# Batch 5's softmax exponentials moved ahead of a middle product, batch 6's joined with batch 7's, in the drain of a conv stage

## The reference, cut to what matters

```python
def _route(x2d, gate_w, num_experts, top_k):
    scores = jax.nn.softmax((x2d @ gate_w.T).astype(jnp.float32), axis=1)
    top_scores, sel = jax.lax.top_k(scores, top_k)
...
    routed_in = (x2d[token_idx].astype(jnp.float32) * top_scores[:, None]).astype(x.dtype)
...
            h = jax.nn.silu(xe @ w1[e]) * (xe @ w3[e])
            out = out + h @ w2[e]
...
x = _layernorm(x + _L0_attn_ref(x, ...), axis=-1)
x = _layernorm(x + _L0_ffn_ref(x, ...), axis=-1)
x = _layernorm(x + _L1_attn_ref(x, ...), axis=-1)
x = _layernorm(x + _L1_ffn_ref(x, ...), axis=-1)
```

## Time and profile before

| | us |
|---|---|
| median of 3 runs | 357.55 |
| lowest, highest | 356.74, 360.23 |
| span of the profiled execution | 349.4 |
| PE busy | 315.8 (90% of the span) |
| DVE busy | 252.3 (72%) |
| ACT busy | 192.7 (55%) |
| POOL busy | 154.6 (44%) |

### The profile page before, as it was taken

How to read it: one execution, slowest core, us unless ns; L and a number is a source line. 1 busy time by engine, 2 the same in 40 slices (tenths; PEclk the granted TensorE clock), 3 DMA queues, 4 the chain that set the end, 5 groups by cost and what they waited for, 6 DMA issues and landing times.

```text
span 349.4 us, 9149 instructions
## 1 busy us (share of the span) xinstructions
PE 315.8 (90%) x2896; PEld 285.2 (82%) x2896; DVE 252.3 (72%) x850; ACT 192.7 (55%) x401; POOL 154.6 (44%) x225
## 2 busy tenths in 40 slices
PE   2989999979689999998977899999889999999992
PEld 2878989868678999998975677777678999999992
DVE  3748988874888568678772589888995787667744
ACT  3154776644464455454536456664557766767342
POOL 0014577862465745876588645312120433134210
PEclk9999999996699999999999699999999999999999
DMA  7991001120134725222501300000000000000001
GB/s 189 421 406 57 17 31 34 38 64 23 46 76 112 234 62 181 63 60 58 160 25 33 122 0 4 2 3 4 1 2 0 3 15 16 15 15 0 18 18 34
DMA packets 17052, 23.24 MB, mean 67 GB/s; under 512 B 3440, under 2 KB 14448, under 8 KB 16224
## 3 DMA queue, kind: packets, MB, share of 16 engines
q1 hardware_dynamic: 14016, 17.84, 16.7%
q0 software_dynamic: 2272, 4.69, 4.0%
q10 hardware_dynamic: 720, 0.14, 0.2%
HBM read 16.93 MB, written 6.73 MB: 68 GB/s over the span
## 4 chain that ended last, share of the span: by engine, by line
PE 55%; DVE 13%; issue 4%; ACT 3%; POOL 2%; DMA 1%; POOLq 0%; DVEq 0%; SPq 0%
PE ps L2015 8%; PE ps L2016 8%; PE ps L1642 6%; PE ps L1845 5%; PE ps L1644 4%; PE ps L1643 4%; PE ps L2079 3%; PE ps L1834 3%; PE ps L1959 2%; PE ps L1937 2%; PE ps L1946 2%; PE ps L1976 2%; DVE sb_stage L1343 1%; DMA out<-sb_work 1%; ACT sb_stage L752 1%
## 5 line engine op out<-in xcount | busy, mean ns | idle before, releaser
L2015 PE MATMUL ps<-sb_w_hi,sb_fh_hi 128*128 128x256 f32 x256 | 61.2, 283 | 1.3 <-DVE sb_w_lo L932 0.6
L2016 PE MATMUL ps<-sb_w_lo,sb_fh_hi 128*128 128x256 f32 x256 | 59.8, 278 | 0.0
L2015 PEld LDWEIGHTS ps<-sb_w_hi,sb_fh_hi 128*128 128x128 f32 x256 | 48.2, 188 | 2.4 <-issue 1.1
L2016 PEld LDWEIGHTS ps<-sb_w_lo,sb_fh_hi 128*128 128x128 f32 x256 | 48.2, 188 | 0.0
L479 POOL DMA_INDIRECT routed<-sb_rows_of,sb_row x32 | 32.3, 1010 | 16.6 <-issue 10.2
L1642 PE MATMUL ps<-sb_w_hi,sb_rT_hi 128*128 x78 | 30.2, 387 | 4.8 <-ACT sb_stage L752 2.7
L619 POOL TENSOR_TENSOR sb_w_lo<-sb_x_in,sb_w_hi 128x256 fp32r<-128x256 f32 x24 | 17.5, 757 | 34.9 <-DVE sb_w_hi L1586 34.9
L1845 PE MATMUL ps<-sb_w,sb_stage 128*128 x234 | 32.8, 276 | 0.0
L571 POOL DMA_INDIRECT answers<-sb_stage x24 | 24.0, 999 | 15.3 <-ACT sb_stage L758 9.4
L1845 PEld LDWEIGHTS ps<-sb_w,sb_stage 128*128 128x128 f32 x234 | 29.2, 191 | 0.2
L463 POOL TENSOR_TENSOR sb_veps_h<-sb_mv_h,sb_eps 128x2 f32<-128x2 f32 x16 | 4.6, 285 | 53.7 <-DVE sb_mv_h L945 48.3
(11 more groups left out here) (301 smaller groups left out, 930.2 us busy)
## 6 DMA issues: line engine op xcount, KB each, us to landing
sb_stage<-in_w SPq DMA_DIRECT2D x2, 1408.0 KB, 13.8
sb_stage<-routed SPq DMA_DIRECT2D x24, 65.0 KB
sb_w<-in_w SPq DMA_DIRECT2D x1, 1536.0 KB, 20.0
sb_x_in<-in_x_tok SPq DMA_DIRECT2D x1, 1024.0 KB, 9.5
sb_x_in<-in_ff_h SPq DMA_DIRECT2D x1, 1024.0 KB
sb_xT_in<-in_ff_h SPq DMA_DIRECT2D x1, 1024.0 KB
sb_got_first<-answers SPq DMA_DIRECT2D x4, 256.0 KB, 3.7
sb_w<-answers SPq DMA_DIRECT2D x4, 256.0 KB, 3.3
```

The source lines that it names most:

```text
L2015: mm(dst, w_hi, x_hi, start=start, stop=False)
L2016: last = mm(dst, w_hi, x_lo, start=False, stop=stop and exact)
```

## The change

It does four things. The two buffers get halves, `below_of[:, b % 2]` and `exps_by[:, b % 2]`, and the waits that guard them become one batch looser. On ACT `exps_of(5)` goes from behind gate row 0 to behind high row 0, with a Silu of one element behind it, and `exps_of(6)` goes from behind `x1_of(6)` to just ahead of `exps_of(7)`. On DVE `weigh(5)` goes from behind `residual(7)` to ahead of `gated_row(0)`, and `weigh(6)` from behind `first_shares()` to behind `share_rest()`. On POOL the four scatters of batch 5 go ahead of `first_root(7)`. PE's and SP's lists are as they were. The new line at 763 moves the lines of ACT and DVE behind it on by one.

```diff
@@ -198,8 +198,8 @@
-        below = sb("below", [P, TILES, EXPERTS])
-        exps = sb("exps", [P, TILES, EXPERTS])
+        below_of = sb("below", [P, 2, TILES, EXPERTS])
+        exps_by = sb("exps", [P, 2, TILES, EXPERTS])
@@ -511,8 +511,8 @@
             first_root(6)
+            scatter_some(5, range(0, 4))
             first_root(7)
-            scatter_some(5, range(0, 4))
@@ -712,8 +712,8 @@
                     act.wait_ge(g0["below"], b + 1)
-                    wait(act, g0["score"], b)
-                    nc.scalar.activation(exps[:, :, :], below[:, :, :], ACT.Exp).then_inc(g0["exps"], 1)
+                    wait(act, g0["score"], b - 1)
+                    nc.scalar.activation(exps_by[:, b % 2, :, :], below_of[:, b % 2, :, :], ACT.Exp).then_inc(g0["exps"], 1)
@@ -759,13 +759,13 @@
             hidden_rows(7)
             high_row(0)
+            exps_of(5)
+            nc.scalar.activation(touched[:, :], ones[:, 0:1], ACT.Silu)
             mid_of(7)
             high_row(1)
             gate_row(0)
-            exps_of(5)
             high_row(2)
             x1_of(6)
-            exps_of(6)
             gate_row(1)
@@ -774,6 +774,7 @@
             high_row(5)
+            exps_of(6)
             exps_of(7)
             gate_row(4)
@@ -1052,8 +1053,8 @@
-                wait(dve, g0["exps"], b)
-                V.tensor_tensor(below[:, :, :], top[:, :, :], top[:, :, 0:1].to_broadcast([P, TILES, EXPERTS]),
+                wait(dve, g0["exps"], b - 1)
+                V.tensor_tensor(below_of[:, b % 2, :, :], top[:, :, :], top[:, :, 0:1].to_broadcast([P, TILES, EXPERTS]),
@@ -1356,9 +1357,9 @@
             low_row(1)
+            weigh(5)
             gated_row(0)
             residual(7)
-            weigh(5)
             low_row(2)
@@ -1370,7 +1371,6 @@
             first_shares()
-            weigh(6)
             low_row(4)
@@ -1379,6 +1379,7 @@
             place(7)
             share_rest()
+            weigh(6)
             gated_row(4)
             turned_row(2)
             weigh(7)
```

More of the change, by code:

```diff
@@ L1223, in weigh @@
                 dve.wait_ge(g0["exps"], b + 1)
-                V.reduce_sum(denom[:, :], exps[:, :, :], axis=AX.X).then_inc(g0["weigh"], 1)
+                V.reduce_sum(denom[:, :], exps_by[:, b % 2, :, :], axis=AX.X).then_inc(g0["weigh"], 1)
                 dve.wait_ge(g0["weigh"], 2 * b + 1)
@@ L1227, in weigh @@
                 dve.wait_ge(g0["weigh"], 2 * b + 2)
-                V.tensor_tensor(rows_by_k[:, b, :, :, AT_SCORE], exps[:, :, 0:TOP_K],
+                V.tensor_tensor(rows_by_k[:, b, :, :, AT_SCORE], exps_by[:, b % 2, :, 0:TOP_K],
                                 rdenom[:, :].unsqueeze(2).to_broadcast([P, TILES, TOP_K]), ALU.mult).then_inc(g0["score"], 1)
```

## The result

The changed kernel takes **362.44 us** (median of 4 runs, 360.70 to 364.55) and the kernel before, in the same rounds, 357.14 us (353.03 to 360.23). The ratio is 1.019 with a 95% interval of 1.011 to 1.027: slower, by about 5 us. The forecast was 356.5, in a range of 354.9 to 358.9. The profiled execution spans 360.7 us and took 362.56.

The account below looks back on a forecast made before the run. VectorE was taken to bound the conv drain, with ScalarE's gate row not setting the pace. Terms -1.06 + 0 + 0, about -1.1, applied to the 357.55 us median gave 356.5, in a range of 354.9 to 358.9.

Parts of the forecast that it names:

- Basis: Whole kernel: summed change applied to the 357.55 us median of runs, 8.15 above the 349.4 us profiled span.
- Exponentials of batch 5 ahead of the middle product: ScalarE, 76.69 to 79.69 us: two table loads, exponentials and touch make `mid_of(7)` 0.25 late; taken as 0.
- Gate row 1, up product 2: Drain on ScalarE and TensorE: gate row near 86.5 instead of 89.27, product near 87.35 instead of 90.02; not the gain.
- Low row 3 bound by VectorE: Drain on VectorE: stays at 90.39 behind work that nothing shortens, so the 2.7 us at TensorE is no gain.
- Term 1, the rank product's wait: VectorE at 92.25 us: its 1.06 us wait for TensorE's batch 6 rank product goes; -1.06, bounds 0 to -1.54.
- clock rival: TensorE's clock low from 92 to 100 us, giving 357.5 (chance 0.18), or still low at 101, giving 359.3 to 361.1 (0.07).
- PE's level eats the gain: TensorE's clock low from 92 to 100 us slows products and transposes, leaving gain 0: 357.5 us, chance 0.18.
- Scatters of batch 5 ahead of root 7: GpSimd from 82.0 us: root begins 0.6 to 1.1 late, its reader ready near 88.2; 0, at worst +0.1.
- Scatters of batches 6 and 7: GpSimd, 100.6 to 109.5 us, at most 110.8: later, but landed by 112 to 113.2, before the 114.4 load; price 0.
- The slower one: TensorE's clock stays low past up product 5, at 101 us, for one or two expert steps: 359.3 to 361.1, chance 0.07.
- Late scatters hold row tile 15: SyncE's load 15 slips if the last scatter lands after about 114.4; 3 us late would end at 359.5, chance 0.03.
- the rivals near 357.5: Cases where no gain remains: low clock (0.18), gain given back or never there (0.10), a drain behind each table load (0.02).

Follow-up runs that it names:

- whole_b: The changed kernel, unchanged, run beside the kernel before on a second chip of the second kind: 362.24 us, ratio 1.0192.
- pool_back: The changed kernel with root 7 ahead of batch 5's scatters on GpSimd again, chip of the second kind: 361.55 us, 1.0195 of the kernel before.
- whole: The changed kernel, unchanged, run again on a chip of the second kind: 362.92 us, 1.0235 of the kernel before.
- burst8: The kernel before plus one GpSimd wait, so batches 6 and 7 push eight in a row; second kind of chip: 362.71 us, 1.0164.
- late6_b: The kernel before with buffer halves and batch 6's exponentials and weighing late, batch 5 as before; second kind of chip: 361.86 us, 1.0183.
- again_b: The kernel before, unchanged, on a chip of the second kind: 356.09 us, 1.0026.
- again: The kernel before, unchanged, on a chip of the first kind: 348.10 us, 1.0015.
- halves: The kernel before with only the buffers' halves and looser waits, all orders as before; first kind of chip: 347.75 us, 1.0005.
- before_gaps: The kernel before plus GpSimd waits for a down product at every second of the first 15 answers' pushes: 357.21 us, 1.0021.
- whole_gaps: The changed kernel plus GpSimd waits between batch 6's and 7's pushes and among the answers' pushes: 359.96 us, 1.0105 of the kernel before.
- whole_pairs: The changed kernel plus GpSimd pauses of about 1.5 us after every second push of batches 6, 7 and first 15 answers: 363.11 us, 1.0236.
- the two parts: The kernel before with buffer halves plus batch 5's edits alone, or batch 6's alone; first kind of chip: 347.80 us (1.0023) and 347.86 us (0.9992).
- early5: The kernel before with buffer halves and batch 5's exponentials, weighing and scatters early, batch 6 as before; first kind of chip: 347.80 us, 1.0023.
- late6: The kernel before with buffer halves and batch 6's exponentials and weighing late, batch 5 as before; first kind of chip: 347.86 us, 0.9992.
- before_pairs: The kernel before plus GpSimd pauses of about 1.5 us after every second push of batches 6, 7 and first 15 answers: 358.18 us, 1.0075.

## Why the prediction was wrong, step by step

- **Basis.** The prediction added the median's distance to the profiled span, 8.15 us, to its sum. That was no constant. In the later runs the time is 1.8 to 2.0 us above its own span (362.56 and 360.7 after); the other 6.3 are most likely the difference of two kinds of chips, since the profile shows no held signal and the runs' times are those of the second kind. The forecast moved a sum made on one kind of chip to the other, and only the sum of the first was worked out. The starting point itself was good (357.55, and 357.14 in the rounds of the result); what failed is the change's own sum, -1.1 for about +5.3.
- **Exponentials of batch 5 ahead of the middle product: right.** Worked out 79.69 for `mid_of(7)` against 79.30 measured, with the whole stretch 0.3 us early. The touch took 0.20, a load 1.28, and the next instruction came 0.01 to 0.02 behind it. The Trainium skill (ScalarE: Activation LUTs, "What ACT_TABLE_LOAD costs") would add a drain of about 1.38 to each load; it is not there.
- **Gate row 1, up product 2: right.** 85.34 for 86.5, and 86.45 for 87.35; the gap of 2.72 is 0.43.
- **Low row 3 bound by VectorE: right in kind.** It came at 89.66, not at 90.39, and row transpose 4 at 90.08 instead of 90.8, waiting 1.49 for it.
- **Term 1, the rank product's wait: right that it goes, not shown as a gain.** VectorE read it at 91.22 with no idle time. Up product 6 is at 101.30 where 102.3 was forecast and 103.39 was before: -2.1 instead of -1.06, of which 0.3 was there at the drain's start and 0.4 more came with low row 3. Most of it goes with TensorE's level, as the last point but one of this list shows.
- **TensorE's level:** 1.00 granted in 100 to 103, and from 82.9 to 106.8 without a break, so in this execution neither clock rival happened up to there. In `whole_b` it is 0.50 from 90.3 to 97.1, which is the rival "PE's level eats the gain". In the changed kernel it is 0.50 again from 106.8 to 117.0, after TensorE had stood for 2.54 us behind a held signal; the step from row transpose 9 to 10 takes 3.9 us there, for 2.8 before. So about 1 us of the loss goes with the level, as a consequence of the hold.
- **Scatters of batch 5 ahead of root 7: right in the places, wrong in "0, at worst +0.1".** First at 81.55 (82.0 forecast), root 7 at 86.40, ending at 87.40, and its reader `first_norm(7)` starts at 87.43. The prediction took the reader to be ready only near 88.2, as before. When the stretch ahead of it runs quicker, the reader is ready first, and the root, behind four pushes, is what it waits for. VectorE in `whole_b`:

```profile
87.63 0.60 DVE L1281 TENSOR_SCALAR sb_rows_of<-sb_work,sb_mv_odd,sb_rstd_odd 128x128 f32<-128x128 f32 x2 [2.42 <-POOL sb_rstd_odd L466]
```

  Six of the ten profiles with the new order have this wait, 1.2 to 2.4 us; none of the ten with the old order has it. In time it can't be told: `pool_back` (1.0195) and `whole` (1.0235) have intervals that overlap.
- **Scatters of batches 6 and 7: the step that failed.** Their places were foreseen well: first at 99.57 for 100.6, last at 108.47 for 109.5. "If the eight then follow each other without the pause between batches" stands in the prediction, and is priced only by when their data must be in. "Price 0" is wrong by the other thing that they do on these chips: while GpSimd pushes without a pause, most signals of TensorE don't land. `burst8` puts the price of joining the two runs of four at 1.64% (0.93 to 2.35), about 5.8 us, and `late6_b` at 1.83%. The changed kernel's whole loss (1.9%, 2.35% and 1.9% in its three measurements) is that, with nothing over that these can tell.
- **The rivals.** The slower one named the clock, and 359.3 to 361.1; the time was over it and by another mechanism. "Late scatters hold row tile 15" had the right instructions and the wrong mechanism: no row transpose waited for them at 114.
- **Where the 2.1 us of the drain went.** They can't be put down to the change. From row transpose 0 to 8 the changed kernel takes 27.7 us and the kernel before 29.4, but TensorE's level is low for 3.4 us of the one and 13.6 us of the other. With as little at the low level, `again_b`, the kernel before, takes 27.3 us; with 10.2 us at the low level four profiles of the old order (`again`, `halves`, `burst8`, `before_gaps`) take 28.6 to 29.7, and three of the new one (`whole`, `whole_gaps`, `whole_pairs`) 28.6 to 30.0. At a like level, then, no lead shows. What lead an execution has on chips of the second kind is then swallowed by the first hold, which ends with the pushes however early TensorE was. On the first kind the two parts, with no hold, gave 1.0023 and 0.9992, no difference that these can tell; the profiles there differ by as much in TensorE's granted clock (0.50 for the 10.2 us from about 88 in `early5`, never in the drain of `late6`), so a gain of 0.3% to 0.6% can be neither shown nor excluded. The whole change was not run on such a chip.
- **Two slips in the working.** High row 5, 1.54 us before 97.05, is at 95.5 and not "about 95.3", so that gate row 4 would be at 98.8; the sum doesn't use it. And the forecast with the rivals near 357.5 adds up to 0.85, not 0.88.

## What stays open

What in GpSimd's pushing holds the signals, and why on three chips of five, isn't settled. One thing goes with it in all 18 runs: where signals are held, the trace also lacks records of semaphore updates, and not only TensorE's. In `again_b` the instructions of the four engines make 151 updates before GpSimd's first indirect DMA at 38.9 us, and all 151 are recorded; of the 863 from there to 4 us behind the last one, at 194.1 us, 690 are; of the 625 after that, all. The updates that DMAs make are 1718 there and 2622 in `again`, the same program on a chip of the first kind, and they too are missing in that stretch alone. With the pauses records still go missing (716 of 887 in `before_pairs`) while nearly no signal is late, so that a missing record and a held signal aren't one thing. So the path by which events are recorded may take part, or may only suffer from the same cause. The Trainium skill (NOTIFIC — the notification-queue block, "7.1 Overflow: three behaviours, one of which stalls the engine") says that this block's internal pipeline always applies back-pressure to what feeds it rather than lose a record inside; no run here shows whether that happens. All the times here come with a recorded span, so none tells how long an execution takes without a record, and it isn't known that the loss would be there.

## What to carry to other kernels

A move that delays one producer can join two bursts of another engine's queue work into one, and the burst's length can matter where no data are late: read the queues' spacing after the move and ask who shares the path, beside when the data must be in. Where the waits name a releaser that no row shows ("remote" on one core), compare the raise of the semaphore with the end of the instruction that makes it before looking for a dependence. And compare kernels only on one chip: two kinds here were 7 to 9 us apart, more than the change, and a sum made from a profile belongs to the chip of that profile. Before you call a lead between two profiles a gain, compare how long TensorE's clock was at its low level in each.

## What the runs showed of the hardware that I had not expected

- On three chips of five, TensorE's signals landed up to 7.6 us after its work in the changed kernel's profile (8.1 in `whole`), in order and then four within 0.2 us. That was 1.0 us after the last push of a run of four (`again_b`) and 1.7 us after the last of eight (changed kernel, `late6_b`, `burst8`), with pushes 1.26 us apart. In a run of pushes one such signal gets through now and then (105.40 and 107.53 in the changed kernel); with 1.5 us of arithmetic behind every second push nearly all do, and no wait of that kind over 1.1 us is left.
- The same program takes 348 us on two chips and 355 to 357 on three others. The kernel before has 11.5 us of waits behind held signals on one of the latter (`again_b`) and none on one of the former (`again`). Not all of them are on the path that sets the end.
- Semaphore updates go unrecorded on those three chips only while GpSimd issues indirect DMAs, whichever engine makes them.
- A pause of 1.5 us after every second push, in a queue that seemed to have time, came back tens of us later as one wait of 9.4 us for a ring load.
